# A two-layer block on one core: attention divided within the experts, mixing written out in rings of three, and the last layer's expert shares worked out in its first MLP

## The reference

```python
# layer 0
xn = layernorm(x)
x  = x + attention(xn)            # 16 heads, 4 kv heads, causal; out @ Wout + bout
       + moe0(xn)                 # top 2 of 8 experts with capacity; gates sum to 1
# layer 1
xn = layernorm(x)
x  = x + pattern_attention(xn)    # 16 heads on 32 learnt patterns, sparsemax; out @ Wo + bo
       + moe1(xn)

def moe1(xn):
    scores = sigmoid(xn @ gate_w.T + lb_bias)
    topw, topi = top_k(scores, 2);  topw = topw / (topw.sum(-1) + 1e-8)
    out = 0
    for e in range(8):
        m     = topi == e
        wmean = (topw * m).sum() / max(m.sum(), 1)      # one number per expert, over all tokens
        out  += where(m.any(-1), mlp_e(xn) * wmean, 0)
    return out + mlp_shared(xn)
```

## Time and profile before

| | us |
|---|---|
| median of 3 runs | 2279.63 |
| lowest, highest run | 2269.03, 2282.21 |
| profiled execution, its own time | 2277.82 |
| its span, first to last instruction | 2275.8 |

### The profile page before, as it was taken

One profiled execution on the slowest core, in us unless ns is written; L12 is line 12 of the kernel. 1 busy time (PEld: TensorE's weight loads), 2 busy tenths in 40 slices (PEclk: granted clock), 3 DMA queues, 4 the chain that ended last, 5 costly groups with the idle time before them and its releaser, 6 DMA issues. The chain is left out here.

```text
span 2275.8 us, 36321 instructions
## 1 busy us (share of the span) xinstructions
PE 2041.2 (90%) x11618; PEld 1224.9 (54%) x11650; DVE 1575.5 (69%) x3508; ACT 984.8 (43%) x2128; POOL 514.2 (23%) x944
## 2 busy tenths in 40 slices
PE   7869999999999999999499999957728999999998
PEld 3322333333333333332399999945515777777777
DVE  5659998888888888882333333327737899999993
ACT  2222667777777677778344544411111111111112
POOL 2450123322222222222233333346500000000000
PEclk9656999999999999999799999976658999999998
DMA  4445001111111111100522232125430000000005
GB/s 137 141 166 188 27 22 65 58 46 42 43 42 43 41 43 44 41 12 11 158 84 89 89 103 95 52 65 154 146 119 22 19 19 19 19 19 10 10 10 162
DMA packets 124881, 152.22 MB, mean 67 GB/s; under 512 B 12952, under 2 KB 111904, under 8 KB 123808
## 3 DMA queue, kind: packets, MB, share of 16 engines
q1 hardware_dynamic: 85584, 99.48, 13.5%
q10 hardware_dynamic: 31440, 29.62, 3.9%
q0 software_dynamic: 7680, 20.98, 2.9%
HBM read 89.29 MB, written 60.29 MB: 66 GB/s over the span
## 5 line engine op out<-in xcount | busy, mean ns | idle before, releaser
L703 ACT ACTIVATE at_wt<-at_B 128x512 f32<-128x512 f32 (+3 forms) x1280 | 606.1, 538 | 251.1 <-PE at_B L753 244.3
L954 DVE TENSOR_REDUCE at_piece_max<-at_A 128x1 f32<-128x512 f32 x768 | 487.3, 683 | 52.7 <-PE at_A L734 50.8
L771 PE MATMUL at_O<-at_wt,at_v 128*32 128x512 f32 (+3 forms) x2560 | 312.3, 540 | 0.0
L657 POOL TENSOR_SCALAR_AFFINE_SELECT at_wt<-at_wt 128x128 f32<-128x128 f32 x512 | 148.0, 294 | 667.1 <-ACT at_wt L703 658.5
L734 PE MATMUL at_A<-at_k,at_q 96*128 96x512 bf16 (+3 forms) x800 | 275.3, 353 | 8.5 <-DVE at_piece_max L951 2.4
L951 DVE CUSTOM_DVE_ANT_0 at_junk<-at_A,at_hide 128x128 bf16<-128x128 f32 (+3 forms) x512 | 230.7, 487 | 73.0 <-PE at_A L734 69.1
L753 PE MATMUL at_B<-at_q,at_k 99*128 99x512 bf16 (+3 forms) x800 | 273.1, 349 | 5.2 <-ACT at_wt L703 5.2
L1392 PE MATMUL ex_H<-ex_xT,ex_w_in 128*128 128x256 f32 x1920 | 247.7, 285 | 3.2 <-DVE ex_xT L1499 3.2
L1392 PEld LDWEIGHTS ex_H<-ex_xT,ex_w_in 128*128 128x128 f32 x1920 | 236.8, 193 | 3.6 <-DVE ex_w_out L1504 3.6
L1513 DVE TENSOR_TENSOR ex_h<-ex_act_a,ex_H 128x256 f32<-128x256 f32 x160 | 67.2, 420 | 226.8 <-ACT ex_act_a L1441 226.7
L734 PE MATMUL at_A<-s_k,s_q 96*128 96x512 bf16 (+2 forms) x480 | 175.8, 384 | 21.5 <-PEq L93 10.6
(11 more groups left out here) (251 smaller groups left out, 2739.0 us busy)
## 6 DMA issues: line engine op xcount, KB each, us to landing
buf<-s_down ACTq DMA_DIRECT2D x10, 1024.0 KB, 11.0
ex_x<-buf SPq DMA_DIRECT2D x40, 256.0 KB, 2.7
expert_out<-ex_y ACTq DMA_DIRECT2D x40, 256.0 KB, 2.1
ex_raw_in<-in_W_in SPq DMA_DIRECT2D x8, 1024.0 KB, 5.0
q_parts<-parts SPq DMA_DIRECT2D x16, 384.0 KB, 4.8
x<-in_x SPq DMA_DIRECT2D x8, 512.0 KB, 4.5
xn<-xn SPq DMA_DIRECT2D x8, 512.0 KB, 5.3
at_v<-v SPq DMA_DIRECT2D x16, 256.0 KB, 3.5
```

The costliest lines, as they stand in the source:

```text
L657: pool.affine_select(block_, block_, [[1, P]], ALU.is_ge, 0.0, base=0, channel_multiplier=-1).then_inc(hidden, 1)
L703: act.activation(wt[(HP * p + h) % NE_][:, q0:CH], pB_of(p, h, u)[:, q0:CH], ACT.Exp, scale=D ** -0.5).then_inc(wt_ready, 1)
L771: pe.matmul(pO[j % 2][rows, q0:CH], vs[n % 3][:, kt // TPC, kt % TPC, :], wt[(HP * p + h) % NE_][:, q0:CH], start=kt < 2 and not late, sto ...
L954: ins = dve.tensor_reduce(top, pA[slot % NA][:, 0:w], AX.X, ALU.max)
```

## The change

- **Division in the experts.** After the last `h` of each of the first nine blocks of `experts`, DVE makes the inverse denominators (block 0) and divides two tiles twice (blocks 1 to 8), in place and packed (`normal_rows`).
- **Mixing written out.** No loop with registers; x, gathered rows and x1 are in rings of three. POOL only issues gathers, with slots and gates read in place. `bout` and `bo` become products of a ones matrix with rows that hold the bias in three bf16 parts (made by POOL in `layer1_weights`, loaded by two more DMAs). The layer norm's last step goes to ACT. The turned xn stays in SBUF (`token_columns`), so neither its store nor its reload is left; the base is stored by SP, not ACT. Bias, maximum and index of the logits are made by DVE in each step, three steps behind.
- **No weighting stage.** Its steps stand in `layer1`: the choice and the mask beside the first scores, the shares before the first MLP's `h`, the means and the scaled weights after it. PE has a product for the sums between its first and second MLP. The mask is no longer spread by DMAs: four products of 128 columns with one column of `neg_ident`, broadcast, take the place of one of 512.
- **Columns for the scores** are copied by ACT, eight copies of 128x128 a chunk, into `xT_score`.
- **Base.** The down products of a chunk begin with two bias products.

The core of the diff:

```diff
+def normal_rows(s):
+
+    return s["attn"][:].rearrange("p t h n -> p (t h n)")[:, 0:TILES * E].rearrange("p (t e) -> p t e", e=E)
+
+
+def token_columns(s):
+
+    return normal_rows(s).rearrange("p (t k) n -> p t k n", k=EC)
...
+                        if f == FC - 1 and first:
+                            divide(i)
+
+            def divide(i):
+
+                if i == 0:
+                    dve.reciprocal(over_sum[:], s["attn"][:, :, :, D]).then_inc(sums_inverse, 1)
+                elif i <= TILES // 4:
+                    dve.wait_ge(sums_inverse, 1)
+                    for pair in (2 * i - 2, 2 * i - 1):
+                        both = slice(2 * pair, 2 * pair + 2)
+                        wait(dve, divided, pair)
+                        dve.tensor_tensor(normal_rows(s)[:, both].rearrange("p t (h n) -> p t h n", n=D),
+                                          s["attn"][:, both, :, 0:D],
+                                          over_sum[:, both].unsqueeze(3).to_broadcast([P, 2, H, D]),
+                                          ALU.mult).then_inc(divided, 1)
 
...
+                wait(pool, sums, SUMS * (t - NR + 1))
+                        c = k * TILES + 2 * t + w
+                            out=ye[k][t % NR][:, w, :], out_offset=None, in_=d["expert_out"],
+                            in_offset=bass.IndirectOffsetOnAxis(ap=s["slot_get"][:, c:c + 1], axis=0),
+                        ).then_inc(rows_in[t % NR], 16)
...
+                wait(pe, sums, SUMS * (t - 2) + 1)
+                pe.matmul(pW[u][:].rearrange("p w e -> p (w e)"), s["ones_bf"][:],
+                          s["bias_rows"][:, 0].rearrange("p w e -> p (w e)"), start=True, stop=False)
...
+            for t in range(STEPS + 2):
+                if t < STEPS:
+                    project(t)
+                if t >= 2:
+                    route(t - 2)
+                    logits(t - 2)
...
+            def normal(t):
+                u = t % 2
+                act.wait_ge(norm, NORM * t + 5)
                 act.activation(std[:], var_eps[:], ACT.Sqrt).then_inc(std_ready, 1)
+                act.wait_ge(norm, NORM * t + 8)
+                wait(act, xnT_made, t - 1)
+                for w in range(2):
+                    act.activation(xn[u][:, w], x1[t % NR][:, w], ACT.Identity, bias=shift[u][:, w:w + 1],
+                                   scale=rstd[u][:, w:w + 1]).then_inc(xn_ready, 1)
...
+            for t in range(STEPS + 2):
+                if t < STEPS:
+                    turned(t)
+                if 1 <= t <= STEPS:
+                    normal(t - 1)
+                if t >= 2:
+                    columns(t - 2)
...
+            for t in range(STEPS + 3):
+                if t < STEPS:
+                    total(t, 0)
+                if t >= 3:
+                    choose(t - 3, 0)
+                if t < STEPS:
+                    total(t, 1)
+                if t >= 3:
+                    choose(t - 3, 1)
+                if t < STEPS:
+                    total(t, 2)
+                if t >= 3:
+                    choose(t - 3, 2)
+                if t < STEPS:
+                    for k in range(5):
+                        normal(t, k)
...
-            for t in range(TILES):
-                c = t // TPC
-                rows = slice(32 * (c % NQ), 32 * (c % NQ) + NX)
-                cols = slice((c // NQ * TPC + t % TPC) * P, (c // NQ * TPC + t % TPC + 1) * P)
-                act.dma_start(s["unsel"][rows, cols], unselT[t % 16 * NX:(t % 16 + 1) * NX, t // 16, :],
-                             allow_slow_non_contiguous=True).then_inc(s["unsel_in"], 16)
...
-                    ins = pe.matmul(pG[i % 2][:], s["neg_rows"][:, c % NQ, e, :], s["unsel"][:, c // NQ * CH:(c // NQ + 1) * CH],
-                                    start=False, stop=True)
+                    for w in range(TPC):
+                        row = (c % NQ * TPC + w) * NX + e
+                        ins = pe.matmul(pG[i % 2][:, w * P:(w + 1) * P], s["neg_ident"][:, row:row + 1].to_broadcast([P, P]),
+                                        unsel[:, c // NQ, :], start=False, stop=(w == TPC - 1))
...
+                    for q in range(PD):
+                        pe.matmul(pD[q][:].rearrange("p w e -> p (w e)"), s["ones_bf"][:],
+                                  s["bias_rows"][:, 1].rearrange("p w e -> p (w e)"), start=True, stop=False)
...
+                    if c == 0 and i == 0:
+                        pe.wait_ge(ones_ready, 1)
+                        pe.wait_ge(unsel_ready, 1)
+                        pe.wait_ge(share_step, SUMMED)
+                        pe.matmul(pO[:, 0:2 * NX], ones[:], expert_sums.rearrange("p a e -> p (a e)"),
+                                  start=True, stop=True).then_inc(summed, 1)
...
+            def columns(c, k):
+
+                wait(act, z_made, TPC * c)
+                cols = xT[:, c // NQ * 8:(c // NQ + 1) * 8, k].rearrange("p t (r j) -> p j t r", j=QT)
+                for t in range(TPC):
+                    ins = act.copy(xT_score[:, k, t].rearrange("p (t r) -> p t r", r=16), cols[:, c % NQ * TPC + t])
+                ins.then_inc(score_cols, 1)
...
+            dve.memset(ones[:], 1.0).then_inc(ones_ready, 1)
+            pick()
+            keep_scores(0, 0)
+            mask()
+            low(0)
+            for t in range(1, TPC):
+                keep_scores(0, t)
+            shares()
...
+                    if c == 0 and i == 0:
+                        means()
```

More of the change, by code:

```diff
@@ L15 @@
+import math
 from contextlib import ExitStack
@@ L1987, in layer1, with early @@
         wT = [sb(f"wT{i}", [P, 4, P]) for i in range(2)]
+        iota = sb("iota", [P, NX])
+        ones = sb("ones", [P, P])
+        mean = sb("mean", [P, NX])
+        starts = [0]
+        def early(*shape):
+            n = math.prod(shape)
+            starts.append(starts[-1] + n)
+            ap = order[1][:, starts[-2]:starts[-1]]
+            if len(shape) == 2:
+                return ap.rearrange("p (a b) -> p a b", a=shape[0])
+            if len(shape) == 3:
+                return ap.rearrange("p (a b c) -> p a b c", a=shape[0], b=shape[1])
+            return ap
+        expert, score, share = (early(TOPK, TILES) for _ in range(3))
+        chosen = early(TOPK, TILES, NX)
+        both, both_eps, inv = (early(TILES) for _ in range(3))
+        picked, shared_sum = (early(TILES, NX) for _ in range(2))
+        expert_sums = early(2, NX)
+        count, inv_count = (early(NX) for _ in range(2))
+        unsel = sb("unsel", [P, B, P], BF16)
         pG = [pb(f"G{i}", [P, CH]) for i in range(2)]
@@ L2173, in silu @@
                 act.activation(act_g[i % 2][:], pG[i % 2][:], ACT.Silu).then_inc(act_ready, 1)
+            for k in range(EC):
+                columns(0, k)
             high(0)
+            for k in range(TOPK):
+                act.activation(score[:, k], s["top"][:, :, k], ACT.Sigmoid).then_inc(scored, 1)
             for c in range(NCH):
@@ L2260, in _ @@
             dve.wait_ge(seg_ready, 1)
-            low(0)
-            for t in range(TPC):
-                keep_scores(0, t)
             for c in range(NCH):
```

531 lines of the change are left out of this document (221 added, 310 removed).

## The result

The changed kernel takes 2192.14 us (median of 4, 2188.78 to 2200.62) where the kernel before took 2277.22 in the same job: ratio 0.9638 [0.9606, 0.967] (the quotient of the two medians is 0.9626). The profiled execution is the fastest, 2188.78 us with a span of 2187.1, so between the two traces lie 89.0 us. The forecast was 2215 with 2195 as its lower end: the sign and the places were right, the gain more than a third larger than its sum of 64.6.

What follows compares the result with a forecast made beforehand. It took PE's chain to bound a mixing step, with POOL 10% on top, and sought the gain in mixing and weighting. Terms 1+0-36.4-39.4+3.5+6.7 = -64.6 took 2277.8 to 2213.2, plus 1.8 for the median: 2215 us, range 2195 to 2246.

Steps and rivals of the forecast that it cites:

- What sets a mixing step: Mixing, kernel before: PE's chain at a mixed clock, 7.4 us, plus 0.7 waiting for POOL's division, near the measured 8.29.
- The steps' term: Mixing's fifteen steps after the change: 7.1 us each, between 7.4 (clock share as before) and 6.7 (half at full clock).
- The floor of 6.0: Mixing after the change: at full clock the logits also wait behind DVE and ACT, so no step under 6.0 us.
- rival (a): Mixing at full clock because PE's row is dense enough: steps of 6.0 us, kernel 2199 us; chance 0.15.
- The front: Last layer, start to first sort: 28.1 us for 24.6, +3.5, with four rounds of product and copy at 4.6.
- weighting's -39.4: The stage between mixing and the last layer goes whole, its DMAs not replaced: -39.4 us.
- the head: Mixing's start to the first product's sum: 9.6 us for 22.0, as PE needs only w_out and the small lb_bias.
- Loop: Last layer's chunks: a bias pair of 0.44 and four exposed masks at +0.1, 0.84 us a chunk, +6.7 in all.
- Experts: Expert stage: DVE's added reciprocal and sixteen products are covered by PE's work: 0, up to 4 us if POOL is late.
- rival (e): Experts: POOL waits out both of DVE's divisions, 1.4 us in eight blocks: +11 us, kernel 2226 us; chance 0.04.
- Weights: Weights stage: two more DMA issues on SP ahead of the expert weights, +1 us, 0 to 1.5.
- rival (b): Mixing at the low clock level throughout: steps of 8.65 us, -16 us there, kernel 2235 us; chance 0.12.

Runs made afterwards that it cites:

- e1: The kernel before with four extra overwritten bf16 products in TensorE's wait of each mixing step; step 8.04 us, ratio to before 0.9988.
- e14: The changed kernel with mixing's output bias added by VectorE instead of TensorE's bias product; step 6.75 us, ratio to before 0.971.
- e13: The kernel before with attention divided in the experts and TensorE's mixing loop written out; step 7.32 us, ratio to before 0.9906.
- e17: The kernel before with the division in the experts, TensorE's mixing loop written out and four extra products a mixing step; step 6.95 us, ratio to before 0.9843.
- e2: The changed kernel with attention divided on POOL within mixing again, not in the experts; step 6.62 us, ratio to before 0.9681.
- e18: The changed kernel with POOL's division back in mixing and rings of two instead of three; step 7.13 us, ratio to before 0.9723.
- e3: The changed kernel with rings of two instead of three in mixing; step 5.95 us, ratio to before 0.9642.
- e4: The changed kernel with four extra overwritten bf16 products in each mixing step; step 5.51 us, ratio to before 0.9583.
- e16: The changed kernel without the last layer's bias pair and three masks in four; chunk 61.66 us, ratio to before 0.9594.

## Why the prediction was wrong

*What sets a mixing step* failed first, for the kernel before. "PE's chain bounds a step, with POOL 10% on top" was fitted: 7.4 plus 0.7 came near 8.29, and so looked shown. e1 refutes it: what held the old step was the circle through POOL and VectorE. The rows for the circle were in the waits of the kernel before, of which I had read only PE's:

```profile
POOL mx_ye L1634 <- issue: 19.5, 56, 0.5
POOL mx_at_slot L1629 <- DVE mx_x L1754: 19.0, 14, 2.1
```

With POOL's 77.6 us of work that fills 116 of 124.3 us.

In the new kernel PE's chain does bound the step, and the forecast's own price for it at 2.4 GHz, 1.39+1.71+1.39+0.97=5.46, is 0.13 over the 5.33 of a short step. That the sentence holds after the change and not before it is luck.

*The steps' term*, 7.1 us, was mis-sized: 5.72 measured, -38.3 for -21.2. Two parts of its working failed. The level's share was assumed to move from 0.3 to a half, but ten of fifteen steps came out at the length of full clock. And the low step was priced with all of PE's row at 1.2 GHz (8.65), where only the product with W is: 7.0 in the trace, 6.83 in e14. Ten steps of 5.33 to 5.45, four of 6.72 to 7.19 and a first one of 4.42 make the mean of 5.72.

*The floor of 6.0* was unfounded too. It was laid over PE's 5.46 for waits of the logits behind DVE, POOL (5.3) and ACT at full clock. No such wait exists: PE's row closes at 5.33 with the two waits for ACT's copies, and VectorE is busy 4.24 (63.54/15). POOL's 5.3 is near the same number, which makes it easy to take for the floor; the rows above speak against it. So rival (a), given 0.15, came nearest, two thirds of the steps at full clock and each 0.7 us shorter than it had them: 2199 for 2192, two errors that partly cancel. The lower end of the range stood on that 6.0.

*The front*, +3.5, came out at -2.2. Three rounds of scores at 4.6 us took 2.77, as the clock was full from 1620.84 (before, their products took 3.68 to 3.79 us for 1.98, the 1.2 GHz level): 5.5 us. Against the fronts of e1, e13 and e17 (21.4 to 23.1 for the 24.6 of before's trace) the change is between -0.7 and +1.0, still below the forecast. The rows had shown the low level behind 23 us without a product; I moved the rounds and kept their clock.

*Right:* weighting's -39.4; the head (8.3 for 9.6, reason as given); the tail (12.8 for 11.8). The missing long eps came as announced. *Loop:* +0.5 a chunk for +0.84. With a mask it is 1.80 us for 1.63 from gate's first load to up's (1.70 for 1.52 in the MLPs beside the transposes), but up's loads then end 0.12 sooner (1.28 for 1.40), so a mask costs 0.05 to 0.06; the bias pair is 0.38 for 0.44; and PE's wait for VectorE shrank from 2.8 to 2.6. *Experts:* "0" was 1 to 2 us. From the first product's start to the last output product's, the four comparable traces without the division (before, e1, e2, e18) show 366.2 to 366.6 us, seven with it and without extra products there (after, e3, e4, e13, e14, e16, e17) 367.4 to 368.3. POOL's low halves take 774 ns in the mean for 750, the longest 1274 for 866, so the divisions do meet them as rival (e) had it, but PE hardly waits for them; how the time is lost is open. *Weights:* +3.1 for +1 in the two traces, between +0.8 and +5.4 over all the traces named above: longer in every one that has the two loads ahead of the expert weights, but by how much and why is not shown. One sum of the forecast doesn't come out as printed: with 8.65 for 7.1 in fifteen steps mixing gives -13.2, not -16, so rival (b) was 2238 and not 2235; nothing hangs on it.

## What to carry to other kernels

When a sum of one engine's chain and its waits comes near the measured step, look at every other engine's row closed with its waits as well; a circle through two of them fits the same number, and which it is shows only when one is made faster. Two rows can be nearly full at the same length, as PE's and POOL's at 5.33 us here: the one that bounds is the one that the others wait for, and that moves the step when it is made longer. Before taking a step length from one trace, look at a second trace of the same stage. Where TensorE works in short bursts between waits, price a step at both clock levels and see which products are low in the trace; a product that "hides in the wait" may decide the level. And when a stage moves behind a busy one, its clock moves too.

## What was unexpected of the hardware

An overwritten bf16 product in a wait is worth time: four a step brought the mean clock of mixing from 0.90 (0.87 in e16) to 0.98 and 3 us (6 against e16) in fifteen steps (e4). The changed kernel's steps are bistable, 5.33 us at 1.00 or 7.01 at 0.76, and stay one kind for several steps. The Trainium skill (TensorE: Matmul & The Clock Gate, the part on oscillation) describes a kernel whose TensorE falls back in every wait for a transfer; the trace agrees that the clock falls back again and again, but the waits here are of 0.5 to 0.7 us, for ScalarE's copies, and not for transfers. The same program gained 3.6% where before takes 2277 us and 2.5% where it takes 2314, by delays of 2 to 10 us behind TensorE that I can't explain.
